# Two elementwise clamps moved from VectorE's queue to GpSimd's in the first stage of a recurrence and attention kernel

## The reference

```python
ek = jnp.exp(jnp.minimum(kf, 30.0))
ekv = ek * vf
# forward and reverse scans over time: a = a * decay + ekv_t ; b = b * decay + ek_t
euk = jnp.exp(jnp.minimum(u + kf, 30.0))
num = nf + nb - ekv + euk * vf
den = df + db - ek + euk
base = sigmoid(r) * (num / jnp.maximum(den, 1e-08))
```

## Time and profile before

| | |
|---|---|
| median of 3 runs | 1232.66 us (1231.87 to 1236.02) |
| profiled execution | 1236.57 us, span 1234.0 us |
| VectorE busy | 901.1 us, 73% of the span |
| GpSimd busy | 410.7 us, 33% |
| ScalarE busy | 597.6 us, 48% |
| TensorE busy | 1018.6 us, 83% |

### The profile page before, as it was taken

The page is one execution under the profiler, slowest core; times in us unless marked ns, Lnnn a source line. Parts: engine busy times, 40 slices in busy tenths (PEclk is TensorE's granted clock), DMA queues, the critical chain, the costliest instruction groups (busy, mean ns, idle before and its releaser), DMA issues. The chain is left out here.

```text
span 1234.0 us, 15885 instructions
## 1 busy us (share of the span) xinstructions
PE 1018.6 (83%) x4848; PEld 570.6 (46%) x4848; DVE 901.1 (73%) x954; ACT 597.6 (48%) x1000; POOL 410.7 (33%) x204
## 2 busy tenths in 40 slices
PE   2776677767766777898999999998889899999995
PEld 0332233333322333265666666665326565555552
DVE  7999999999999972145556566565224687777885
ACT  4666776677667761024555555556203333333222
POOL 3776767667666750000111111111000032233333
PEclk9888988888799888999999999999799999999998
DMA  3332323223232316594335344331558566757553
GB/s 106 108 131 102 114 107 126 112 102 119 104 134 102 119 52 256 220 345 129 117 119 170 124 156 153 119 119 69 230 236 331 175 205 211 255 203 263 198 195 128
DMA packets 83377, 196.33 MB, mean 159 GB/s; under 512 B 6803, under 2 KB 48915, under 8 KB 80277
## 3 DMA queue, kind: packets, MB, share of 16 engines
q1 hardware_dynamic: 83348, 195.97, 44.8%
HBM read 137.22 MB, written 58.73 MB: 159 GB/s over the span
## 5 line engine op out<-in xcount | busy, mean ns | idle before, releaser
L362 PE MATMUL bank<-work,ident 128*128 128x512 f32 x384 | 222.1, 709 | 51.2 <-POOL work L338 23.1
L916 PE MATMUL bank<-work 128*128 (+1 forms) x1024 | 246.3, 384 | 8.3 <-PEq L495 4.4
L940 PE MATMUL bank<-work 128*128 (+1 forms) x512 | 232.0, 596 | 2.6 <-ACT work L1040 1.8
L916 PEld LDWEIGHTS bank<-work 128*128 128x128 f32 x1024 | 188.3, 191 | 47.1 <-issue 26.6
L1095 POOL TENSOR_TENSOR work<-work 128x1024 f32<-128x1024 f32 x32 | 75.1, 2347 | 290.3 <-DVE work L1022 290.3
L1085 POOL COPY xres<-work 128x1024 f32 (+1 forms) x32 | 33.3, 1040 | 373.2 <-DVE work L1022 373.2
L362 PEld LDWEIGHTS bank<-work,ident 128*128 128x128 f32 x384 | 76.8, 221 | 157.6 <-issue 77.3
L940 PEld LDWEIGHTS bank<-work 128*128 128x128 f32 x512 | 97.7, 191 | 99.1 <-issue 92.9
L371 PE MATMUL bank<-ident,work 128*128 128x128 f32 x256 | 46.7, 342 | 96.8 <-DVE work L314 96.8
L974 DVE TENSOR_TENSOR work<-bank,sbias 128x256 f32<-128x256 f32 x64 | 27.2, 425 | 124.9 <-PE bank L916 124.9
L338 POOL TENSOR_TENSOR work<-work 128x1024 f32<-128x1024 f32 x32 | 75.9, 2373 | 120.6 <-DVE work L305 120.6
(11 more groups left out here) (152 smaller groups left out, 1604.9 us busy)
## 6 DMA issues: line engine op xcount, KB each, us to landing
work<-in_kT SPq DMA_DIRECT2D x32, 512.0 KB, 3.3
work<-in_xT SPq DMA_DIRECT2D x32, 512.0 KB, 4.2
x0T_scratch<-work SPq DMA_DIRECT2D x32, 512.0 KB, 2.6
work<-x0T_scratch SPq DMA_DIRECT2D x32, 512.0 KB, 4.0
x1T_scratch<-work SPq DMA_DIRECT2D x32, 512.0 KB, 2.6
work<-x1T_scratch SPq DMA_DIRECT2D x32, 512.0 KB, 4.2
work<-in_x_nat SPq DMA_DIRECT2D x32, 512.0 KB, 4.2
out<-work SPq DMA_DIRECT2D x32, 512.0 KB, 2.9
```

Source lines behind the costliest of these rows:

```text
L362: last = nc.tensor.matmul(ps_num[p][:, cols], ident[:], v[:, cols], start=(k == 0), stop=(k == 2), skip_group_check=True)
L916: last = nc.tensor.matmul(ps_s[p], xTb[p][:, c, :], Amat[:, i, :, c * 32:c * 32 + 32], start=(c == 0), stop=(c == NC - 1))
L940: last = nc.tensor.matmul(ps_o[:, cols], attT[:, k * P:(k + 1) * P], Bmat[k][:, i, cols], start=(k == 0), stop=(k == 1), skip_group_check= ...
```

## The change

The two clamps leave VectorE. The clamp of exp(k) at a cap is replaced by a clamp of k at 30 ahead of the exponential, on GpSimd, from `kbuf` to `ek`; the exponential then works in place on `ek`, which now has two buffers (`ekr` is gone). The clamp of exp(-r) stays behind its exponential and is done on GpSimd. Both are put into GpSimd's queue behind its second addition of a tile: first the clamp of exp(-r) of this tile, then the clamp of k of the next tile. All five engines now run stage 1 as straight code, where `over_tiles` made a loop (`for n in range(NT + 2): body(n, n % 2)` and the like).

```diff
-        ekr = cut(3072, T)
-        ek = cut(4096, T)
+        ek = [cut(1024 * i, T) for i in (3, 4)]
...
                 def exp_k(n, p):
+                    wait(act, kc_ok, n + 1)
+                    nc.scalar.activation(ek[p], ek[p], ACT.Exp).then_inc(ek_ok, 1)
+
+                def exp_uk(n, p):
                     wait(act, k_in[p], (n // 2 + 1) * 16)
-                    wait(act, ek_ok, n)
-                    nc.scalar.activation(ekr, kbuf[p], ACT.Exp).then_inc(ek_raw, 1)
-
-                def exp_uk(n, p):
...
             def _(dve):
...
                     if exists(n):
-                        wait(dve, ek_raw, n + 1)
-                        wait(dve, df_ok, n)
-                        nc.vector.tensor_scalar(ek, ekr, EXP_CAP, None, ALU.min).then_inc(ek_ok, 1)
-                    if exists(n - 1):
-                        wait(dve, er_raw, n)
-                        nc.vector.tensor_scalar(rbuf[1 - p], rbuf[1 - p], ER_CAP, None, ALU.min).then_inc(er_ok, 1)
-                    if exists(n):
                         wait(dve, ek_ok, n + 1)
                         wait(dve, nb_ok, n)
-                        nc.vector.tensor_tensor(ekv, ek, kbuf[p], ALU.mult).then_inc(ekv_ok, 1)
+                        nc.vector.tensor_tensor(ekv, ek[p], kbuf[p], ALU.mult).then_inc(ekv_ok, 1)
...
             def _(pool):
                 constants_pool(pool)
+
+                def cap_k(n, p):
+                    wait(pool, k_in[p], (n // 2 + 1) * 16)
+                    wait(pool, df_ok, n - 1)
+                    nc.gpsimd.tensor_scalar(ek[p], kbuf[p], EXP_MAX, None, ALU.min).then_inc(kc_ok, 1)
...
                         wait(pool, sum1_ok, n + 1)
                         nc.gpsimd.tensor_tensor(den[p], den[p], delta[p], ALU.add).then_inc(den_ok, 1)
-
-                over_tiles(pool, body, 1)
+                        wait(pool, er_raw, n + 1)
+                        nc.gpsimd.tensor_scalar(rbuf[p], rbuf[p], ER_CAP, None, ALU.min).then_inc(er_ok, 1)
+                    if exists(n + 1):
+                        cap_k(n + 1, 1 - p)
+
+                cap_k(0, 0)
+                for n in range(NT + 1):
+                    body(n, n % 2)
```

More of the change, by code:

```diff
@@ L22 @@
 TQ = T // Q
+EXP_MAX = 30.0
 EXP_CAP = 10686474581524.463
@@ L206, in build @@
         x0_out = csem("x0_out")
-        ek_raw, eu_raw, er_raw = csem("ek_raw"), csem("eu_raw"), csem("er_raw")
+        kc_ok, eu_raw, er_raw = csem("kc_ok"), csem("eu_raw"), csem("er_raw")
         ek_ok, er_ok, ekv_ok, delta_ok = csem("ek_ok"), csem("er_ok"), csem("ekv_ok"), csem("delta_ok")
@@ L231, in _ @@
                 constants_sp(sp)
-                over_tiles(sp, body, 2)
+                for n in range(NT + 2):
+                    body(n, n % 2)
                 sp.wait_ge(x0_out, 16 * NT)
@@ L282, in body @@
                                              ACT.Copy).then_inc(nat_ev, 1)
-                over_tiles(act, body, 2)
+                for n in range(NT + 2):
+                    body(n, n % 2)
             @block.vector
@@ L292, in body @@
                     if exists(n):
-                        wait(dve, ek_raw, n + 1)
-                        wait(dve, df_ok, n)
-                        nc.vector.tensor_scalar(ek, ekr, EXP_CAP, None, ALU.min).then_inc(ek_ok, 1)
-                    if exists(n - 1):
-                        wait(dve, er_raw, n)
-                        nc.vector.tensor_scalar(rbuf[1 - p], rbuf[1 - p], ER_CAP, None, ALU.min).then_inc(er_ok, 1)
-                    if exists(n):
                         wait(dve, ek_ok, n + 1)
                         wait(dve, nb_ok, n)
-                        nc.vector.tensor_tensor(ekv, ek, kbuf[p], ALU.mult).then_inc(ekv_ok, 1)
+                        nc.vector.tensor_tensor(ekv, ek[p], kbuf[p], ALU.mult).then_inc(ekv_ok, 1)
                         wait(dve, eu_raw, n + 1)
                         wait(dve, den_ok, n - 1)
-                        nc.vector.scalar_tensor_tensor(delta[p], eur, EXP_CAP, ek, ALU.min, ALU.subtract)\
+                        nc.vector.scalar_tensor_tensor(delta[p], eur, EXP_CAP, ek[p], ALU.min, ALU.subtract)\
                             .then_inc(delta_ok, 1)
@@ L318, in body @@
                         wait(dve, sum1_ok, n)
-                        nc.vector.tensor_tensor_scan(db[:, ::-1], dec, ek[:, ::-1], 0.0, ALU.mult, ALU.add)\
+                        nc.vector.tensor_tensor_scan(db[:, ::-1], dec, ek[p][:, ::-1], 0.0, ALU.mult, ALU.add)\
                             .then_inc(db_ok, 1)
                         wait(dve, x0_ok, n - 1)
-                        nc.vector.tensor_tensor_scan(den[p], dec, ek, 0.0, ALU.mult, ALU.add).then_inc(df_ok, 1)
+                        nc.vector.tensor_tensor_scan(den[p], dec, ek[p], 0.0, ALU.mult, ALU.add).then_inc(df_ok, 1)
                         wait(dve, ekv_ok, n + 1)
@@ L327, in body @@
                             .then_inc(nb_ok, 1)
-                over_tiles(dve, body, 3)
+                for n in range(NT + 3):
+                    body(n, n % 2)
             @block.gpsimd
@@ L394, in body @@
                         numerator(nb, nb_ok, num_ok, 2)
-                over_tiles(pe, body, 2)
+                for n in range(NT + 2):
+                    body(n, n % 2)
         CH = C // 2
```

## The result

The changed kernel takes 1431.97 us (median of 4 runs, 1429.68 to 1433.58) against 1233.3 before: a ratio of 1.161 with a 95% interval of 1.159 to 1.164. It is slower by 198.7 us. Forecast were 1320 us and a range of 1309 to 1350. The side was right; the forecast loss of 87.7 us is less than half of the measured one.

A forecast was written before the change was run, and what follows sets the result against it. VectorE's queue was taken to bound stage 1; the new ring makes 31 pitches 515.0 us against 427.4 (+87.6), first tile -0.6, drain +0.7, net +87.7 on 1232.66: 1320 us, range 1309 to 1350.

The forecast's parts named there:

- What bounds the kernel: Stage 1 is bound by VectorE's own queue, 13.86 us a tile, 12.20 once the two clamps are off.
- the faster rival: Stage 1: VectorE stays the bound, 51 us come off, time 1181 us; chance 0.03 for this side.
- the half microsecond: Stage 1, VectorE: the part of clamp L295 spent waiting for GpSimd's L348, said to go with the clamp.
- The ring: Stage 1: next exp(k) waits for the k clamp behind GpSimd's additions, which need this tile's results; tile 13.86 to 16.75 us.
- the price of a clamp: Each of the two GpSimd clamps in stage 1 taken at 1.04 us, like a one-input copy.
- the bound from above: Upper end for a GpSimd clamp: a two-input operation of the same size (L348), 2.35 us.
- the drain: End of stage 1 after the last tile: L255 starts 14.7 us after L302 instead of 13.97, +0.7 us.
- The rival of the dearer clamp: GpSimd clamps in the ring cost more than a copy: 1361 us at 1.7, 1401 at 2.35; chance 0.12.
- The estimate from the page: GpSimd clamp by the Trainium skill's 1.8 cycles an element: about 1.54 us, time about 1351 us.
- The unrolling: Stage 1 as straight code instead of a loop: costed at nothing.
- The signs: Stage 1 profile after: L338 idle about 3.5 us, L342 1.6, L346 none, VectorE about 4.5; clamps near 1.04.

The follow-up runs named there:

- quick clamps: Changed kernel with both GpSimd clamps, in the same places, written as two-operation min then max: 1327.59 us, ratio 1.078.
- the copies: Changed kernel with both GpSimd clamps replaced by GpSimd copies of the same size in the same places: 1318.67 us, ratio 1.069.
- the loop version: Kernel before with VectorE's output product moved ahead of its two clamps, stage 1 still a loop: 1226.82 us, ratio 0.995.
- in straight code: Kernel before with VectorE's output product moved ahead of its two clamps and stage 1 as straight code: 1225.07 us, ratio 0.993.

## Why the prediction was wrong

- **What bounds the kernel** was right: VectorE's queue. With the clamps off it and nothing in its way, the tile is 12.19 us where 12.20 was worked out, and the kernel gains the 51 us of the faster rival. That took a third engine for the clamps and the output product in front; no version with a clamp on GpSimd came near it (1226 us at best). The prediction let the half microsecond in which L295 waits for GpSimd go with the clamp. It doesn't go by itself: with the output product behind the delta, as in the change, the ekv product waits in its place, and the tile is 12.68 us. In the slow ring this cost nothing.
- **The ring** was right in order and nearly in size. With 1.04 us operations in the clamps' places the kernel took 1319 us (1320 forecast) and the tile 16.62 (16.75). Even with quick clamps the change as placed costs 94 us.
- **The failed step is the price of a clamp**: "Not below 1.04 [...] I take 1.04, as the clamp has one input like the copy", and the bound from above, the two-input 2.35. It measured 2.76, outside both. Two clamps in the ring make 2 x (2.76 - 1.04) = 3.44 us a tile: 16.75 + 3.44 = 20.19, measured 20.23. That this agrees to 0.04 us is in part luck: against the copies the slow clamps add 3.61 us a tile, since the k clamp also starts after the end of the other (2.85 us from start to start, where the copies have 0.97 for 1.04), and the ring was forecast 0.13 too long. Times 31 the 3.44 us are 107 of the missing 111 us; most of the rest lies behind the last ekv product (797.3 us to the end of the span against 794.2, +3.1 where +0.7 was forecast), and the drain has a clamp in it too. A two-input operation that adds says nothing about the upper end of a one-input operation that takes a minimum. The rival of the dearer clamp named the mechanism, with too low a ceiling (1401) and a chance of 0.12.
- **The estimate from the page** (1.54 us) was nearer and still 1.2 us short. The Trainium skill (GPSIMD Engine Reference, Engine selection) calls one-input work roughly line rate; the runs bear that out for the copy and the quick pairs (1.04 us) and not for one operation alone (2.76).
- **The clamp of exp(-r)** alone makes some 75 us of the loss, as the version with only the k clamp shows.
- **The unrolling** costs nothing: measured, 1.001.
- **The signs** named ahead: L339 idle 3.56 (3.5), L343 idle 1.62 (1.6), no wait ahead of L347. All came. VectorE's wait (7.94 instead of 4.5) and the clamps' own duration showed the failed term.

## What to carry to other kernels

An engine with idle time isn't a free place for work: ask which queue the moved instruction then stands in, and whether the bound engine's next tile waits for its end. Prefetched work that is put behind the consumer's own results closes a ring, and every instruction in it is paid in full. And a price must be measured for the very operation on the very engine, since here a second, idle operation made a clamp 2.7 times quicker.

## What the runs showed of the hardware

- On GpSimd, 128x1024 fp32 tensor_scalar: one operation (min, mult or add) 2.76 to 2.78 us, 2.84 with its bound in a column; min then max, mult then add, mult then mult 1.04; min then min, max then min 3.63. A copy takes 1.04, a two-input multiplication 2.34.
- VectorE's two-input instructions and GpSimd's operations block each other in both directions, an instruction at a time: 2.39 and 3.37 us instead of 1.21 on VectorE, 3.33 and 3.22 instead of 2.36 on GpSimd. VectorE's one-input clamp waits for GpSimd in the same way (1.88 us instead of 0.68). Its scans and its output product, which read PSUM besides, take their usual 2.26 and 1.27 us beside GpSimd's operations.
- A wait that a profile leaves without a releaser ("issue") isn't safely issue time. Ahead of the output product, 17 waits of the loop version had none (4.8 us); in straight code 13 of the like name TensorE (4.6 us) and one has none. In both they stand in the tiles in which the numerator's first matmuls ran at the lower level of TensorE's clock (3.78 us instead of 1.98), and the kernels take nearly the same time.
